# Attention phase: VectorE folds the weights ahead of the sums with x, and ScalarE's copies change places

## The reference, cut to what matters

```
def _autocorrelation(Q, K, V):                   # Q = layernorm(x), K = V = ctx
    q, k, v = ...                                # 8 heads of 256 channels
    qf = fft(q, axis=tokens); kf = fft(k, axis=tokens)
    corr = ifft(qf * conj(kf)).real              # per channel: 256 lags
    w, idx = top_k(corr, 11)                     # the 11 best lags
    w = softmax(w)
    out = sum over i of w[i] * v[min(idx[i] + pos, 255)]
```

## Time and profile before

| what | value |
|---|---|
| median of 3 runs | 3191.58 us (3190.05 to 3197.46) |
| profiled execution | 3189.48 us, span 3187.7 us |
| busy over the span | PE 91%, DVE 86%, ACT 71%, POOL 50% |
| mean granted TensorE clock | 0.972 of full speed (2.4 GHz); 1.00 from 143 to 1203 us |

### The profile page before, as it was taken

The page is one execution under the profiler, slowest core; times in us unless marked ns, Lnnn a source line. Parts: engine busy times, 40 slices in busy tenths (PEclk is TensorE's granted clock), DMA queues, the critical chain, the costliest instruction groups (busy, mean ns, idle before and its releaser), DMA issues. The chain is left out here.

```text
span 3187.7 us, 47981 instructions
## 1 busy us (share of the span) xinstructions
PE 2911.0 (91%) x13554; PEld 1586.1 (50%) x13554; DVE 2737.9 (86%) x7168; ACT 2252.5 (71%) x5963; POOL 1581.7 (50%) x1161
## 2 busy tenths in 40 slices
PE   5999999999999996899999999999999999738886
PEld 3666666666666663445444454444445444322322
DVE  4999999999999996776878879787887978769996
ACT  6888888888888862765766767667586766468773
POOL 5999999999999992001212121121212212016776
PEclk8999999999999998999999999999999999859998
DMA  5555555555555535354654737465473744553664
GB/s 174 185 188 167 180 174 161 181 173 160 178 178 160 177 117 173 87 163 126 177 169 136 225 110 214 131 178 163 136 225 103 206 148 132 124 194 147 247 250 162
DMA packets 272044, 532.26 MB, mean 167 GB/s; under 512 B 32664, under 2 KB 132760, under 8 KB 248992
## 3 DMA queue, kind: packets, MB, share of 16 engines
q1 hardware_dynamic: 245600, 422.17, 42.4%
q10 hardware_dynamic: 15168, 71.34, 7.9%
q0 software_dynamic: 11008, 35.66, 3.3%
HBM read 401.07 MB, written 128.02 MB: 166 GB/s over the span
## 5 line engine op out<-in xcount | busy, mean ns | idle before, releaser
L1065 PE MATMUL acc<-xh,wq 128*128 128x512 f16 x4096 | 1205.7, 381 | 46.3 <-DVE x_first L1722 17.1
L1065 PE MATMUL acc<-xl,wq 128*128 128x512 f16 x2048 | 758.9, 380 | 0.0
L1284 ACT ACTIVATE unused<-c_first,minus_guess 128x256 bf16<-128x256 f32 x1024 | 505.2, 494 | 268.5 <-DVE minus_guess L1596 224.5
L1065 PEld LDWEIGHTS acc<-xh,wq 128*128 128x128 f16 x4096 | 399.4, 98 | 532.9 <-DVE x_first L1722 23.3
L994 POOL DMA_DIRECT2D c_first<-ctx_pairs x120 | 66.5, 554 | 857.3 <-DVE mk L1647 846.9
L1065 PEld LDWEIGHTS acc<-xl,wq 128*128 128x128 f16 x2048 | 200.8, 98 | 243.3 <-issue 2.7
L444 PEld LDWEIGHTS bu<-m_iz,zf 128*128 128x128 f32 x2048 | 278.9, 191 | 50.3 <-issue 35.6
L444 PE MATMUL bu<-m_iz,zf 128*128 128x128 f32 (+2 forms) x2048 | 293.0, 301 | 5.5 <-DVE zf L648 5.5
L463 PE MATMUL bx<-m_ic,pf 128*128 128x256 f32 x1024 | 236.1, 384 | 8.9 <-POOL pf L345 8.9
L463 PEld LDWEIGHTS bx<-m_ic,pf 128*128 128x128 f32 x1024 | 192.7, 193 | 34.1 <-POOL pf L345 9.7
L1266 ACT ACTIVATE unread<-cf 128x256 bf16<-128x256 f32 x256 | 106.1, 415 | 127.9 <-DVE feat_pair L1695 94.9
(11 more groups left out here) (359 smaller groups left out, 6975.9 us busy)
## 6 DMA issues: line engine op xcount, KB each, us to landing
wq<-w_split SPq DMA_DIRECT2D x512, 256.0 KB, 3.2
c_first<-ctx SPq DMA_DIRECT2D x64, 512.0 KB, 7.4
xt<-xT SPq DMA_DIRECT2D x64, 512.0 KB, 5.9
x_pairs<-xo SPq DMA_DIRECT2D x64, 512.0 KB, 3.3
c_first<-ctx_pairs POOLq DMA_DIRECT2D x128, 256.0 KB, 4.8
x<-xn_pairs SPq DMA_DIRECT2D x32, 1024.0 KB, 5.4
out_pairs<-ost SPq DMA_DIRECT2D x32, 1024.0 KB, 5.1
x_first<-x SPq DMA_DIRECT2D x15, 2048.0 KB, 8.4
```

The lines of the kernel that those rows point to most:

```text
L1065: return pe.matmul(acc[b][:], ws[(WQ * o + k // CK) % WR][:, k % CK, a, :], x[:, k, :], start=start, stop=False)
L1284: act.activation(signs[:, u // 2, t] if n == COUNTS - 1 else unused[u % 2][:], ct[k % CR][:, t], ACT.Sign, bias=guess[q % 2][:, u:u + 1], ...
```

## The change

It reorders instructions on two engines and adds or removes none. On ScalarE, `w_back` moves ahead of the row sums `w_rows`, and the second half of the correlation copies moves ahead of the squares of x1. On VectorE, the fold of the weights moves from behind the four sums with x to ahead of them, and so ahead of all that these wait for.

```diff
@@ ScalarE, in step
                 squares(it, k, 0)
+                if t is not None:
+                    act.wait_ge(t_mm, t + 1)
+                    if least(t, 1):
+                        act.wait_ge(fold_ok, 2 * t)
+                    act.activation(wb[:], by[:, 1, :], ACT.Copy).then_inc(wb_sb, 1)
                 h = chunk(it, k, AFTER_W + 1)
                 if h is not None:
                     w = wn[h % 2]
                     act.wait_ge(wn_in[h % 2], 16 * (h // 2 + 1))
                     act.activation(w[:], w[:], ACT.Copy, scale=W_SCALE, accum_out=wrow[:, h:h + 1]).then_inc(w_summed, 1)
-                if t is not None:
-                    act.wait_ge(t_mm, t + 1)
-                    if least(t, 1):
-                        act.wait_ge(fold_ok, 2 * t)
-                    act.activation(wb[:], by[:, 1, :], ACT.Copy).then_inc(wb_sb, 1)
                 if f is not None and least(f, 2):
                     act.wait_ge(w_cut, CT * (f - 1))
                 correlations(f, 0)
+                correlations(f, 1)
                 if g is not None:
                     s = (k - AFTER_I) % 2
                     act.wait_ge(x1_sum, CT * (g + 1))
                     act.activation(xt[s][:], xo[s][:], ACT.Square).then_inc(sq1_ok, 1)
-                correlations(f, 1)
@@ VectorE, in step
                     dve.tensor_tensor(plus, plus, odd, ALU.add).then_inc(joined_ok, 1)
+                if t is not None:
+                    s = (k - AFTER_T) % 2
+                    dve.wait_ge(wb_sb, t + 1)
+                    if least(t, 1):
+                        dve.wait_ge(wo_mm, t)
+                    dve.tensor_tensor(we[:, 0, :], by[:, 0, :], wb[:], ALU.add).then_inc(fold_ok, 1)
+                    dve.tensor_tensor(we[:, 1, :], by[:, 0, :], wb[:], ALU.subtract).then_inc(fold_ok, 1)
+                if g is not None:
+                    kk = k - AFTER_I
+                    s = kk % 2
                     dve.wait_ge(joined_ok, g + 1)
                     dve.wait_ge(xt_in[s], 16 * (4 * it + kk // 2 + 1))
...
                     for j in range(CT):
                         dve.scalar_tensor_tensor(xo[s][:, j, :], ..., xt[s][:, j, :], ALU.mult, ALU.add).then_inc(x1_sum, 1)
-                if t is not None:
-                    s = (k - AFTER_T) % 2
-                    dve.wait_ge(wb_sb, t + 1)
-                    if least(t, 1):
-                        dve.wait_ge(wo_mm, t)
-                    dve.tensor_tensor(we[:, 0, :], by[:, 0, :], wb[:], ALU.add).then_inc(fold_ok, 1)
-                    dve.tensor_tensor(we[:, 1, :], by[:, 0, :], wb[:], ALU.subtract).then_inc(fold_ok, 1)
                 if f is not None:
```

## The result

The changed kernel takes 3200.0 us (median of 20 runs, 3195.8 to 3206.3) against 3191.6 for the kernel before (20 runs): a ratio of 1.0026, 95% interval 1.0019 to 1.0032, so 8.5 us or 0.26% slower. The forecast was 11.7 us slower. The profiled execution took 3198.6 us with a span of 3196.8, 9.1 more than before; at the first instruction of the next phase's split (VectorE, 1248.45 before, 1256.68 after) 8.2 of these are there, so the attention phase holds nearly all of it.

A forecast was written before the change was run, and what follows sets the result against it. Two limits side by side: the loop through TensorE (18.3 us a step) and VectorE's own work (17.84 to 18.28). Terms 8.8 + 9.7 - 3.2 - 3.6 = +11.7 us gave 3203.3 us, 0.37% slower, range 3190 to 3219.

The forecast's parts named there:

- (a): VectorE's fold ahead of the sums: TensorE loop 1.58 us shorter, no longer a limit; `prod_o` gates `bz`, only 0.28 earlier.
- The rival without any lead: ScalarE and TensorE come no earlier against VectorE (`xo` at 11.2 or later in M and Q): +23 us, chance 0.13.
- (b): ScalarE's `w_back` gains only 0.61 us, still behind mean and squares; VectorE's fold waits 0.91 in M, 1.43 in Q.
- (c): Step lengths from the fold's start (4.93 us to the end): M 0.63 longer, Q 0.69 longer, V 0.23 shorter, R unchanged.
- M: Attention-phase step kind (k = 1, 5) carrying ScalarE's `mean(.., 0)`; 14 steps, forecast from 18.29 to 18.92 us.
- Q: Attention-phase step kind (k = 2, 6) carrying ScalarE's `squares(.., 0)`; 14 steps, forecast from 18.75 to 19.44 us.
- V: Attention-phase step kind (k = 3, 7) carrying VectorE's variance; 14 steps, forecast from 18.30 to 18.07 us.
- R: Attention-phase step kind (k = 0, 4) carrying VectorE's `scales`; 15 steps, forecast to stay at 18.28 us.
- (d): ScalarE's normalization and next step's head 0.6 to 0.7 us later, GpSimdE and SyncE later too: hidden, nothing taken.
- (e): Phase ends: five last steps without extra work 0.3 us shorter each, last folding step 1.58 earlier, first fold about 0.5.
- The rival of no change: Same fold stalls, but larger gains beside them (TensorE lead of 0.5 or more): 0 to +8 us, chance 0.19.
- The rival of a stall-free gain: TensorE's wait for the fold vanishes and the wait for `w_back` is absorbed: -26 us, 3165.5, chance 0.10.

## Why the prediction was right, step by step

(a) The early fold shortens the loop, and `prod_o` gates what TensorE gains: right, shown by the delay of the gate. The size was off: I had let `bz` start 0.06 behind `prod_o`, the row shows 0.14 to 0.15, and the product itself takes longer after a wait (`bz` to `bu` 1.79 instead of 1.72). So `xo` came to 11.14, not 10.99, and the lead was 0.13 instead of 0.28. The rival without any lead had its border at 11.2: it fell, but about half of its loss came true.

(b), (c) The fold waits in M and Q for a `w_back` that still stands behind mean and squares: right, and shown by putting `w_back` first. M and Q grew by 0.73 and 0.77 (forecast 0.63 and 0.69), the 0.10 being mostly the smaller lead. V shrank by 0.33 (forecast 0.23) and R by 0.21 (forecast nothing). The step that failed is "R: VectorE's own work, 18.28, no change". Two things were hidden in that 18.28: L735 to L743 lay 0.73 apart because the sums depend on L735, and with the fold between them that gap is filled (0.60 in the R rows above); and `prod_e` at 671.26 did not follow MAX8 but TensorE's `we` product, which ended at 669.24 + 1.98 = 671.22. TensorE's timeline of the kernel before shows it:

```profile
669.24 1.98 PE L404 MATMUL by<-w_fold,m_e 128*128 128x512 f32 x4 [0.54 <-DVE w_fold L750]
```

I called the step VectorE's own because the view listed no wait; but a gap as small as the 0.12 before the first `wk` (606.16 + 1.21 = 607.37 to 607.49 in the kernel before) stands in no list. In V the wait for `xo` did not give way to the variance either: L733 starts 651.96 - 640.19 = 11.77 into the step, 0.63 behind `xo` as in M, where 11.68 was written.

(d) The late head on ScalarE: right. In R, `kf` starts at 663.46 - 658.16 = 5.30, the value written, and the first `wk` at 10.08 does not wait. GpSimdE's longer wait for the squares and SyncE's later store reached nobody: in the list of waits the only other engine that waits for GpSimdE is TensorE, once, for 0.2 us, and none waits for a DMA.

(e) The five bare steps gained 0.32 each, the last fold's step 1.3 (20.13 to 18.80). In that step the fold came 1.7 earlier, and some of it was lost again because TensorE's product behind it took longer (3.78 against 3.41, with a granted clock of 0.50 against 0.57). For the first folds I had estimated 0.5. The first `prod_e` does come 2.4 earlier (63.92 before, 61.49 after), but this is not the change's doing. TensorE's first product of the phase starts 0.46 earlier (20.13 and 19.67), ahead of all that was moved; and the first correlations, the same 16 matmuls, took 6.53 and then 5.25 us, with a granted clock of 0.56 and 0.70 over them (first the kernel before, then the changed one):

```profile
37.31 6.53 PE L463 MATMUL bx<-m_ic,pf 128*128 128x256 f32 x16 [8.89 <-POOL pf L345]
```

```profile
36.85 5.25 PE L463 MATMUL bx<-m_ic,pf 128*128 128x256 f32 x16 [10.18 <-POOL pf L345]
```

The second correlations took 5.14 and 4.51. These three make 0.46 + 1.28 + 0.63 = 2.37 of the 2.43, which leaves 0.06 for the change. Over the runs of this document the first `prod_e` lies anywhere between 61.5 and 64.2.

The sum by these sizes: 14 x (0.73 + 0.77 - 0.33) - 15 x 0.21 - 1.6 - 1.3 = +10.3, and with the 2.4 that the clock and the earlier start gave this one execution +7.9, where 8.2 stand at the end of the phase. That 10.3 lies near the forecast's 11.7 is in part luck, as misses of both signs met: M and Q cost 14 x 0.18 = 2.5 more than forecast, V and R gave 1.4 + 3.2 = 4.6 more.

The rival of no change, with its 3192 to 3200, ends just where the median lies. Of its two grounds one holds in part: small gaps closed in V and R. The other, a lead of 0.5 or more, did not come. The rival of a stall-free gain fell: TensorE's wait for the fold did go, from 43.9 to 7.9 us, and the kernel became slower. The Trainium skill's advice on this, to optimize what blocks a matmul engine that idles waiting for others ("Perfetto Trace Analysis", section "Optimization Strategies"), held here only when the engine with the highest share was not made to wait in exchange: with `w_back` first it brought 20 us, without it cost 8.

## What to carry to other kernels

When an instruction is moved ahead on a full engine, look up when its input arrives in each kind of step, not in the typical one: here half of the steps had nothing in front of the copy, and the other half had 1.9 to 2.4 us, of which only Q's wait of 0.37 had shown anything, because the late fold covered the rest. Move the producer first, then the consumer; here each alone was worth little or was a loss. And where two limits stand side by side within 0.5 us of a step, count the gaps that are too short to be listed before calling one of them the engine's own work.

## What of the hardware was not expected

Where TensorE had waited 2.43 us in the run with `scales` ahead, its granted clock went down for the matmuls that followed (stretches of that run; columns as in the earlier trace rows):

```profile
690.90:692.00 1.10, 1.06 (x3) 0.57 (x4) 1.10 (x5) 0.72 (x2) 1.10 (x1) 0.92 0.97 354
692.00:694.00 2.00, 2.00 (x4) 0.93 (x3) 1.91 (x5) 0.14 (x1) 2.00 (x2) 0.50 0.10 35
694.00:696.00 2.00, 2.00 (x10) 1.76 (x9) 1.92 (x2) 1.97 (x5) 1.42 (x2) 0.69 0.00 0
696.00:698.80 2.80, 2.80 (x24) 2.72 (x23) 1.87 (x9) 1.17 (x3) 2.80 (x4) 1.00 0.03 6
```

0.50 is the lower level, 1.2 GHz, against 2.4 GHz at 1.00. `bz` took 2.88 us instead of 1.95 and `bu` 5.37 instead of 4.57 for the same matmuls. In the two R steps of 20.07 us the wait was as long, but the clock stayed up, as the row and the stretches of one of them show:

```profile
301.25 1.96 PE L404 MATMUL bz<-ce,m_o 128*128 128x512 f32 x4 [2.42 <-DVE prod_o L642]
```

```profile
301.23:302.43 1.20, 1.18 (x3) 0.66 (x4) 1.20 (x5) 0.69 (x2) 1.20 (x1) 1.00 0.94 343
302.43:304.43 2.00, 2.00 (x11) 1.48 (x10) 1.91 (x5) 1.19 (x2) 2.00 (x2) 1.00 0.10 36
```

So the fall of the clock cost 21.77 - 20.07 = 1.70 us of a step, and after waits of equal length it came in twelve steps and not in two; what decides between them stays open. Behind the wait of 1.1 us at the same place (`cut_first` ahead) `bz` took 1.95 us, its time at the higher level. The Trainium skill describes such a gate in "TensorE: Matmul & The Clock Gate", section "Part 1: The HAM clock gate"; the two levels in the rows agree with it.
